# Attention outputs in two halves of 256 query columns, interleaved with the scores, and the attention stage's jobs in another order

## The reference

```python
x = x + 0.5 * ffn(layernorm(x))     # 8 experts of 128 -> 256 -> 128, exact gelu, all experts summed, times a gate
x = x + attention(layernorm(x))     # 8 heads of 8 features, q and k of unit length, causal, scale 8
x = x + 0.5 * ffn(layernorm(x))     # the same weights
```

```python
sim = einsum('bhid,bhjd->bhij', q, k) * 8.0
sim = where(causal_mask, sim, lowest)
attn = softmax(sim, axis=-1)
o = einsum('bhij,bhjd->bhid', attn, v)
return o.transpose(...).reshape(b, n, 64) @ w_out
```

## Time and profile before

| | us |
|---|---|
| median of 3 runs | 269.75 (269.66 to 269.92) |
| the profiled execution | 269.82, its span 268.1 |
| PE busy | 258.2 |
| ACT busy | 217.5 |
| DVE busy | 216.2 |
| POOL busy | 80.7 |

### The profile page before, as it was taken

The page is one execution under the profiler, slowest core; times in us unless marked ns, Lnnn a source line. Parts: engine busy times, 40 slices in busy tenths (PEclk is TensorE's granted clock), DMA queues, the critical chain, the costliest instruction groups (busy, mean ns, idle before and its releaser), DMA issues.

```text
span 268.1 us, 5428 instructions
## 1 busy us (share of the span) xinstructions
PE 258.2 (96%) x1829; PEld 183.6 (69%) x1829; DVE 216.2 (81%) x590; ACT 217.5 (81%) x344; POOL 80.7 (30%) x175
## 2 busy tenths in 40 slices
PE   7999999999999999979998999999999999999995
PEld 6886878888788786533434433378888887888783
DVE  7999899998898987797378587378889678697784
ACT  2897668859878889999999999987777867859673
POOL 6302104204850482664349545520200000200100
PEclk9999999999999999999999999999999999999999
DMA  5741200001012104101314003300004211210311
GB/s 152 219 123 23 58 1 2 0 1 39 2 34 46 42 2 78 40 1 22 62 39 82 2 4 78 80 1 4 0 8 111 42 39 39 39 34 9 80 39 39
DMA packets 33343, 11.51 MB, mean 43 GB/s; under 512 B 24130, under 2 KB 32548, under 8 KB 33316
## 3 DMA queue, kind: packets, MB, share of 16 engines
q1 hardware_dynamic: 33172, 11.11, 17.7%
q10 hardware_dynamic: 144, 0.07, 0.1%
HBM read 4.88 MB, written 2.62 MB: 28 GB/s over the span
## 4 chain that ended last, share of the span: by engine, by line
PE 73%; DVE 8%; ACT 7%; issue 5%; POOL 4%; DMA 2%; SPq 0%; POOLq 0%; DVEq 0%; ACTq 0%
PE ps L590 10%; PE ps L596 10%; PE ps L608 10%; PE ps L593 10%; PE ps L613 10%; PE ps L611 9%; PE ps L746 5%; ACT probs L937 3%; PE ps L708 2%; PE ps L777 2%; ACT h L924 2%; POOL probs L1533 1%; POOL w_raw L1527 1%; DMA kT<-k_stack 1%; DVE h_lo L1100 1%
## 5 line engine op out<-in xcount | busy, mean ns | idle before, releaser
L924 ACT ACTIVATE h<-ps,cols 128x512 f32<-128x512 f32 x128 | 88.0, 694 | 36.2 <-PE ps L596 32.6
L1100 DVE TENSOR_TENSOR h_lo<-h,h_hi 128x512 fp32r<-128x512 f32 x128 | 88.6, 698 | 19.1 <-ACT h_hi L927 16.7
L937 ACT ACTIVATE probs<-ps 128x1024 f32<-128x1024 f32 (+1 forms) x80 | 65.0, 918 | 1.5 <-PE ps L708 1.4
L590 PE MATMUL ps<-xT_hi,w_hi 128*128 128x512 f32 x128 | 51.5, 402 | 0.0
L608 PE MATMUL ps<-h_hi,w_hi 128*128 128x512 f32 x128 | 50.5, 395 | 0.3 <-ACT yT L949 0.3
L927 ACT ACTIVATE h_hi<-ps,cols 128x512 fp32r<-128x512 f32 x73 | 50.2, 688 | 0.0
L613 PE MATMUL ps<-h_lo,w_hi 128*128 128x512 f32 x128 | 50.2, 392 | 0.0
L596 PE MATMUL ps<-xT_lo,w_hi 128*128 128x512 f32 x128 | 49.9, 390 | 0.0
L593 PE MATMUL ps<-xT_hi,w_lo 128*128 128x512 f32 x128 | 49.9, 390 | 0.0
L611 PE MATMUL ps<-h_hi,w_lo 128*128 128x512 f32 x128 | 49.9, 389 | 0.0
L746 PE MATMUL ps<-probs,v_ones 128*32 128x512 f32 (+4 forms) x384 | 34.2, 458 | 0.9 <-POOL probs L1533 0.6
(11 more groups left out here) (141 smaller groups left out, 273.2 us busy)
## 6 DMA issues: line engine op xcount, KB each, us to landing
w_raw<-in_L_ffn_w SPq DMA_DIRECT2D x8, 256.0 KB, 4.6
turned<-blocks SPq DMA_DIRECT2D x6, 256.0 KB, 2.0
w_raw<-turned SPq DMA_DIRECT2D x24, 64.0 KB, 2.3
w_raw<-v_ones SPq DMA_DIRECT2D x8, 128.0 KB, 2.4
x_sb<-in_L_attn_x SPq DMA_DIRECT2D x3, 256.0 KB, 6.8
out_x<-x_sb SPq DMA_DIRECT2D x3, 256.0 KB, 2.3
w_raw<-o_scaled SPq DMA_DIRECT2D x2, 256.0 KB, 4.3
x_sb<-in_L_attn_x SPq DMA_DIRECT2D x2, 128.0 KB, 2.3
```

What stands on the lines that cost most here:

```text
L590: pe.matmul(bank, w1_hi[:, w], xT_hi[:, cols_g], start=True, stop=False)
L924: first = nc.scalar.activation(h[:, slot, :], ps[:, BANK_H + slot, :], ACT.Gelu, bias=bias)
L937: nc.scalar.activation(probs[:, s % P_SLOTS, :, 0:width], ps[:, bank:bank + 2, 0:width], ACT.Exp, scale=SCALE).then_inc(exp_done, 1)
L1100: dve.tensor_tensor(h_lo[:, slot, :], h[:, slot, :], h_hi[:, slot, :].bitcast(f32), ALU.subtract).then_inc(split_done, 1)
```

## The change

For k from 3 to 34 (`halved`), the outputs of the last quad behind step k are computed in two halves: its query columns 0 to 255 (`pv(quad, 0)`) between scores 2k and scores 2k + 1, and columns 256 to 511 (`pv(quad, 1)`) after scores 2k + 1. The rule for corner steps (`short`) is gone. Every matmul of `pv` is cut to the columns of its half: a full key tile becomes two times 256 columns, an item of 448 columns from query 64 becomes 192 and 256, and so on. `pv_done` is incremented after the second half. Outside of these steps both halves are issued together.

The jobs change order and place. Before: `ln` at quad 6, `project (0, 0)` at 8, `project (0, 1)` at 10, `qkv 0` at 11, `qkv 1` at 13; after: `ln` at 6, `qkv 0` at 7, `qkv 1` at 10, `project (0, 0)` at 12, `project (0, 1)` at 14. `project (2, 0)` and `(2, 1)` move from quads 28 and 30 to 30 and 32. `ffn_ln`, `project (1, 0)` and `(1, 1)` stay at 23, 25 and 26. DVE's work follows: the stacks of the last group come after `project (0, 0)` is emptied, the FFN's first normalise just before `ffn_ln` is emptied, the second after `project (1, 1)`. POOL's `ln_once(GROUPS)` moves from behind the masks of quad 12 to behind those of quad 19.

```diff
-        jobs = [(q1, "ln", LAST), (q1 + 2, "project", (0, 0)), (q1 + 4, "project", (0, 1)),
-                (q1 + 5, "qkv", 0), (q1 + 7, "qkv", 1), (q2 + 3, "ffn_ln", 0),
-                (q2 + 5, "project", (1, 0)), (q3, "project", (1, 1)),
-                (q3 + 2, "project", (2, 0)), (q3 + 4, "project", (2, 1)),
+        jobs = [(q1, "ln", LAST), (q1 + 1, "qkv", 0), (q1 + 4, "qkv", 1),
+                (q1 + 6, "project", (0, 0)), (q1 + 8, "project", (0, 1)),
+                (q2 + 3, "ffn_ln", 0), (q2 + 5, "project", (1, 0)), (q3, "project", (1, 1)),
+                (q3 + 4, "project", (2, 0)), (q3 + 6, "project", (2, 1)),
                 (quad_steps, "project", (pairs - 1, None))]
...
-            def pv(k):
+            def pv(k, half):
...
                     for n, tiles in parts:
+                        if n != half:
+                            continue
                         for j in range(4):
...
                     for n, (kt, q0, width, at) in enumerate(st["item"]):
+                        first = max(q0, GROUP // 2 * half)
+                        end = min(q0 + width, GROUP // 2 * half + GROUP // 2)
+                        if first >= end:
+                            continue
                         for j in range(4):
-                            m = pe.matmul(ps[ROW * j:ROW * j + ROW, bank, q0:q0 + width],
+                            m = pe.matmul(ps[ROW * j:ROW * j + ROW, bank, first:end],
                                           v_ones[:, SEQ // P * st["b"] + kt, 4 * st["quad"] + j, :],
-                                          probs[:, (s + j // 2) % P_SLOTS, j % 2, at:at + width],
-                                          start=(opens and n == 0), stop=False)
-                m.then_inc(pv_done, 1)
+                                          probs[:, (s + j // 2) % P_SLOTS, j % 2, at + first - q0:at + end - q0],
+                                          start=(opens_bank and n == 0), stop=False)
+                if half:
+                    m.then_inc(pv_done, 1)
...
+            def first_halves_of(k):
+
+                for quad in quads_behind(k)[-1:]:
+                    pv(quad, 0)
+
+            def quads_behind(k):
+                return range(max(pv_until(k - 1), 0), pv_until(k))
+
-            def outputs(k):
+            def outputs(k, begun=False):
...
-                    pv(quad)
+                    if not begun or quad != quads_behind(k)[-1]:
+                        pv(quad, 0)
+                    pv(quad, 1)
...
             for k in range(quad_steps):
-                short = steps[2 * k]["last"] and k < quad_steps - 1
                 if k == PV_LAG - 1:
                     third_products(0)
                 scores_of(2 * k)
-                if short:
-                    outputs(k)
+                halved = PV_LAG <= k < PV_CLOSER
+                if halved:
+                    first_halves_of(k)
                 scores_of(2 * k + 1)
-                if not short:
-                    outputs(k)
+                outputs(k, halved)
...
+                if kind == "ffn_ln":
+                    normalise(FFN, GROUPS, 0)
                 empty(n)
...
-                if (kind, arg) == ("project", (0, 1)):
-                    dve.wait_ge(job_emptied, n + 1)
-                    first_stats(GROUPS)
                 if (kind, arg) == ("qkv", 1):
...
+                if (kind, arg) == ("project", (0, 0)):
                     stacks(LAST)
-                    normalise(FFN, GROUPS, 0)
+                if (kind, arg) == ("project", (0, 1)):
+                    dve.wait_ge(job_emptied, n + 1)
+                    first_stats(GROUPS)
...
                     gate_shift(GROUPS)
-                if (kind, arg) == ("project", (2, 0)):
                     normalise(FFN, GROUPS + 1, 1)
                     turn_features(GROUPS + 1)
+                if (kind, arg) == ("project", (2, 0)):
                     gate_weight(GROUPS)
...
-                if s == 2 * last_quad[2] + 1:
+                if s == 2 * last_quad[3] + 1:
                     ln_once(GROUPS)
```

More of the change, by code:

```diff
@@ L719, in pv @@
                 opens, closes = st["first"] and st["quad"] == 0, st["last"] and st["quad"] == QUADS - 1
-                if opens and pair == 0:
+                opens_bank = opens and half == 0
+                if opens_bank and pair == 0:
                     pe.wait_ge(third_copied, 1)
-                if opens and pair == 1:
+                if opens_bank and pair == 1:
                     pe.wait_ge(resid, GROUP_TILES * GROUPS)
-                if opens and pair > 1:
+                if opens_bank and pair > 1:
                     pe.wait_ge(job_emptied, sum(at < k for at, *_ in jobs))
@@ L817, in scores_of @@
                     scores(s)
-            def outputs(k):
+            def first_halves_of(k):
[4 more added lines that the diff above has]
+            def outputs(k, begun=False):
                 nonlocal next_job
-                for quad in range(max(pv_until(k - 1), 0), pv_until(k)):
+                for quad in quads_behind(k):
                     if quad == quad_steps - 1:
```

## The result

The changed kernel takes 277.09 us (median of 4 runs, 277.05 to 277.19) against 269.77 us: a ratio of 1.0273, 95% interval 1.026 to 1.0286, so 7.3 us slower. The prediction was 276.6, in a range of 272.0 to 279.5.

A forecast was written before the change was run, and what follows sets the result against it. PE becomes the bound for k = 3 to 34: scores 18.8, outputs 33.9, jobs 7.1, sum 59.8 us against ACT's 50.3. With waits and a later hole, exponentials end 6.8 us later: 276.6 us, range 272.0 to 279.5.

The forecast's parts named there:

- Where the bound moves: Attention, k = 3 to 34: PE becomes the bound with 59.8 us against ACT's 50.3, plus 0.3 us of waits.
- Scores apart: k = 3 to 34: separated score steps can't share time, 0.32 us each (0.18 at corners), 18.8 us in all, 8.3 more.
- Outputs in halves: k = 3 to 34: each stretch pays 0.14 us beyond its columns; outputs take 33.9 us, 4.5 more.
- The jobs moved: Jobs' PE cost unchanged, but project (2, 1) leaves the stage: 7.1 us; the k = 26 wait of 0.19 us goes, winning nothing.
- The hole behind k = 35: Scores 72 follow 2.4 us after scores 70, the job at quad 32 included; exponentials end 6.8 us later.
- PE's slack: Before the change, k = 3 to 34: PE's work of 47.6 in 53.4 us leaves 5.8 us of slack.
- rival A: Switches in k = 3 to 34 cost next to nothing, ACT stays the bound and recovers 3.5 us: 266.3; chance 0.07.
- B: Halves of outputs are free, scores apart aren't: PE 55.3 us, time 272.1; chance 0.08.
- C: DVE's 0.5 us of cover at quad 14 fails or masks come late: 1 to 3 us more, 278 to 280; chance 0.10.
- The forecast of 592 records: Records of the outputs' matmuls (L746) go from 384 to 592.

The follow-up runs named there:

- narrow exponentials: From step 16 each wide exponential skips its second 256 columns, in the kernel before with only the jobs' new order (267.30 us) and in the changed kernel (275.88 us).
- halves_adjacent: Changed kernel with matmuls still cut to halves, but both halves adjacent, after the scores (at corner steps between them): 270.18 us, ratio 1.0011.
- narrow_exp_new_jobs: Kernel before with only the jobs' new order, each wide exponential from step 16 on leaving out its second 256 columns: 267.30 us, ratio 0.9906.
- whole_between_scores: Changed kernel with each quad's outputs uncut between the two score steps for k = 3 to 34: 273.93 us, ratio 1.0154.

## Why the prediction was right

**Where the bound moves.** Right. PE's sum for k = 3 to 34 was 59.8 us and 0.3 of waits; measured are 60.51, of which PE waits 0.34 for POOL and 0.20 for DVE. Of the two waits that the 0.3 stood for, at k = 27 and 29, only the second came; the one for POOL's masks at k = 8 was not in the sum. The terms came out singly, not by luck of the sum: added up from start to start, the scores take 19.0 us (forecast 18.8), the outputs 33.9 (33.9) and the jobs 7.0 (7.1). The narrow exponentials show that ACT has no part in it.

**Scores apart, 0.32 us a step.** Right: 0.31 to 0.32, for two records as for four.

**Outputs in halves, 0.14 us beyond the columns.** Right, from the corner quads' 0.57: halves take 0.57 to 0.58, and halves_adjacent shows that it is the switch that costs, not the cut: there the outputs of k = 3 to 34 add up to 29.65 us, in as many records, where the changed kernel takes 33.9. By the Trainium skill, TensorEngine Tiling (Array Packing), Tiling Modes, Key Properties, a change of tiling mode drains the engine; these two kernels, of 270.18 and 277.09 us with the same matmuls, agree. Scores and outputs also differ in type (f16 and f32), and no run tells what of the 0.14 us is due to which.

**The jobs moved.** Right that they hardly matter. The wait for the turned stacks is gone: in the changed kernel SyncE issues the second transposing DMA at 141.19, as its timeline shows, and the scores of k = 26 stand at 152.28 with no wait.

```profile
139.91 1.25 SPq L529 DMA_TRANSPOSE qT<-q_stack  x1
141.19 1.33 SPq L529 DMA_TRANSPOSE kT<-k_stack  x1
```

**The hole behind k = 35.** Right in place, a little small. Forecast were 2.4 us between scores 70 and 72 and exponential 72 6.8 us late; measured 2.54 and 7.3. The job stands between the outputs of quads 32 and 33, so quad 32 pays its own 0.58 and not the 0.46 of two adjoining outputs. That 0.1 us and the 0.4 by which the first stretch is longer make up the difference of 276.6 and 277.1.

**PE's slack.** This step was wrong, though the forecast didn't rest on it. The 5.8 us between sum and span were called PE's slack, and rival A's break-even was put at half of the added cost. Half of the steps halved lost 3.0 us, and 1.3 us is what the narrow exponentials closed up from k = 8 on. In the trace before, PE's timeline from k = 3 to 34 divides the 5.8 us: 3.1 are waits that it names (1.7 for POOL, 0.9 for ACT, 0.4 for DVE, 0.2 for a DMA), and 2.6 are stretches of scores longer than their 0.32 or 0.18 us. The waits for POOL and DVE are no slack that ACT's pace gives back. That three sets of scores keep PE from feeding ACT further ahead may be the rest of it; no run has more sets, so that is argued and not shown.

**The rivals.** A fell with ACT's 7.8 us of idle time, B with the halves' 0.57 us. C's place didn't show: in the changed kernel the second projection at quad 14 stands at 139.03 us without a wait, and PE's waits for masks and DVE are 0.54 us in all from k = 3 to 34, where the kernel before has 2.0. The narrow_exp_new_jobs kernel has C's wait, 0.98 us, where PE isn't slowed by the halves.

**Records.** The forecast of 592 records for the outputs was wrong; there are 640. The cut is in `pv` itself, so it also divides the six quads from 33 on whose halves stand together, 8 records each.

## What to carry to other kernels

Before interleaving two kinds of matmul more finely, price the switch from the trace: take a short and a long stretch of the same kind between the same neighbours, and what doesn't shrink with the columns is the price. Here a further alternation costs 0.46 us, a third of a step, while cutting the matmuls where they stand cost 0.16 us in all. When the engine that issues is within a few per cent of the engine it feeds, don't count the difference between span and sum as room: take work from the engine that is fed in one experiment and see how much the stage closes up.

## What the runs showed of the hardware that was not expected

Two score steps in different groups of 32 rows, issued together, take 0.32 us, and one alone takes 0.31 to 0.32: the second was free only beside the first, and stood at full price once it was apart. A stretch of outputs cut into 24 records instead of 16 keeps its length (1.00 us each, from 127.95 and from 130.13 in whole_between_scores), and so does one cut into 16 instead of 8 (1.00 us, from 172.16 in the changed kernel).
